# Gate, up and router products in plain fp32, with all expert weights resident in SBUF

## What is computed

```
logits = (x @ wt.T + repeat(g @ wg.T)) / 2             # 8 experts
scores = softmax(logits);  topk_w, topk_idx = top_k(scores, 2), normalised
gp = leaky(einsum('th,ehm->etm', x, w_gate))           # H = 256, M = 128
up = einsum('th,ehm->etm', x, w_up)
y_all = einsum('etm,emh->eth', gp * up, w_down)
y = sum of topk_w * y_all over the two chosen experts
p = leaky(x @ sw_gate) * (x @ sw_up) @ sw_down         # shared, width 256
y = y + p
```

## Time and profile before

| | us |
|---|---|
| runs: median, lowest, highest | 1060.24, 1060.23, 1061.74 |
| the profiled execution's own time | 1064.17 |
| its span, first to last instruction | 1062.4 |
| PE busy | 1014.6 (96%) |
| DVE busy | 707.4 (67%) |
| ACT busy | 526.5 (50%) |

### The profile page before, as it was taken

One profiled execution on the slowest core, in us unless ns is written; L12 is line 12 of the kernel. 1 busy time (PEld: TensorE's weight loads), 2 busy tenths in 40 slices (PEclk: granted clock), 3 DMA queues, 4 the chain that ended last, 5 costly groups with the idle time before them and its releaser, 6 DMA issues.

```text
span 1062.4 us, 21427 instructions
## 1 busy us (share of the span) xinstructions
PE 1014.6 (96%) x6788; PEld 815.3 (77%) x6788; DVE 707.4 (67%) x2457; ACT 526.5 (50%) x1564; POOL 437.0 (41%) x422
## 2 busy tenths in 40 slices
PE   3887999999999999999999999999999999999998
PEld 2665877778777887778777787777877788777877
DVE  8789577665867558665676647676576755856543
ACT  3488346651565435663456614665246643565220
POOL 1634154441554333642535515454245534444212
PEclk9899999999999999999999999999999999999999
DMA  5316414112132013311132212311123211232043
GB/s 198 80 54 215 151 60 122 53 66 63 61 110 90 28 55 101 100 61 61 43 118 72 71 42 79 112 65 46 62 66 113 82 41 41 84 106 71 20 138 102
DMA packets 40996, 87.68 MB, mean 83 GB/s; under 512 B 4192, under 2 KB 19040, under 8 KB 40624
## 3 DMA queue, kind: packets, MB, share of 16 engines
q1 hardware_dynamic: 39920, 83.57, 24.5%
q10 hardware_dynamic: 960, 2.62, 0.7%
HBM read 76.57 MB, written 9.60 MB: 81 GB/s over the span
## 4 chain that ended last, share of the span: by engine, by line
PE 75%; DVE 10%; issue 5%; ACT 4%; DVEq 0%; POOL 0%; ACTq 0%
PE psY L1641 13%; PE psS L1511 6%; PE psO L1547 5%; PE psG L69 5%; PE psG L71 5%; PE psG L70 5%; PE psT L1522 5%; PE psS L71 3%; PE psS L70 3%; PE psS L69 3%; PE psS L1507 3%; PE psT L1529 2%; PE psO L1550 2%; PE psT L69 2%; PE psT L71 2%
## 5 line engine op out<-in xcount | busy, mean ns | idle before, releaser
L604 POOL TENSOR_TENSOR work<-work,rden 128x514 f32<-128x514 f32 x128 | 134.0, 1047 | 322.3 <-DVE rden L1137 321.6
L1641 PE MATMUL psY<-Wd,H 128*128 128x256 f32 x640 | 172.5, 399 | 0.0
L763 ACT ACTIVATE work<-work,low 128x257 f32<-128x257 f32 x256 | 128.5, 504 | 60.1 <-DVE low L1155 59.5
L69 PE MATMUL psG<-x1T_hi,Wgu 128*128 128x512 f32 (+1 forms) x292 | 134.8, 462 | 2.6 <-ACT leaky L807 1.9
L1641 PEld LDWEIGHTS psY<-Wd,H 128*128 128x128 f32 x640 | 112.4, 190 | 29.4 <-issue 14.4
L1155 DVE CUSTOM_DVE_ANT_0 work<-psS,bias,null_s 128x256 f32<-128x256 f32 x256 | 113.3, 480 | 28.4 <-PE psS L1511 25.9
L1251 DVE SCALAR_TENSOR_TENSOR leaky<-leaky 128x512 f32<-128x512 f32 x80 | 56.4, 704 | 101.5 <-ACT leaky L807 100.5
L71 PE MATMUL psG<-x1T_lo,Wgu 128*128 128x512 f32 (+1 forms) x292 | 114.9, 394 | 0.0
L70 PE MATMUL psG<-x1T_hi,Wgu 128*128 128x512 f32 (+1 forms) x292 | 114.4, 392 | 0.0
L593 POOL TENSOR_TENSOR rq<-qss,neghalf 128x16 f32<-128x16 f32 x32 | 97.5, 3048 | 36.3 <-DVE qss L1131 36.3
L1511 PE MATMUL psS<-KB,qT 64*128 64x256 f32 (+1 forms) x1024 | 105.7, 325 | 0.0
(11 more groups left out here) (259 smaller groups left out, 2306.7 us busy)
## 6 DMA issues: line engine op xcount, KB each, us to landing
Wgu<-wexp SPq DMA_DIRECT2D x80, 512.0 KB, 3.4
Wb<-wscr SPq DMA_DIRECT2D x64, 256.0 KB, 3.6
wexp<-Wgu SPq DMA_DIRECT2D x10, 512.0 KB, 2.9
xres<-in_x SPq DMA_DIRECT2D x8, 512.0 KB, 4.7
xin<-in_x SPq DMA_DIRECT2D x7, 512.0 KB, 4.2
out<-work SPq DMA_DIRECT2D x7, 512.0 KB, 2.9
H<-in_wgu SPq DMA_DIRECT2D x10, 256.0 KB, 3.9
bias<-bscr SPq DMA_DIRECT2D x4, 512.0 KB, 6.6
```

What stands on the lines that cost most here:

```text
L69: te.matmul(dst, a_hi, b_hi, start=start, stop=False)
L604: pool.tensor_tensor(T1[sl][:, hs, :], T1[sl][:, hs, :], rden[sl][:, 1, hs].unsqueeze(2) .to_broadcast([P, 2, N + 1]), ALU.mult)
L763: act.activation(T1[sl][:, h, :], T1[sl][:, h, :], ACT.Exp, scale=-1.0, bias=low[sl][:, 1, h:h + 1], accum_out=den[sl][:, 1, h:h + 1])
L1641: mm = te.matmul(psY[:, t // 2, (t % 2) * D:(t % 2 + 1) * D], H[:, k % H_RING, t * P:(t + 1) * P], Wd[:, ORDER[k], :], start=(k == 0 and t ...
```

## The change

Gate, up and the router's logits become plain fp32 matmuls. x1T is one fp32 tile: ACT copies its half 0, DVE its half 1. Wgu holds all ten blocks (20 KB per partition) and is loaded once, by ten DMAs of 256 KB straight from the input. The splitting in round 0, `wexp`, `load_weights` and all its waits go; the fp32r copy of the router's weights, the identity sum I2 and the logits' second half of rows go as well. One wait is added on PE, in round 0, behind the query products.

```diff
-        x1T = [sb(f"x1T_{part}", [P, KC, TOK], F32R) for part in PARTS]
-        Wgu = sb("Wgu", [P, W_RING, 2, 2, KC, P], F32R)
+        x1T = sb("x1T", [P, KC, TOK])
+        Wgu = sb("Wgu", [P, BLOCKS, 2, KC, P])
...
-            for e in range(BLOCKS + 2):
-                if e < BLOCKS:
-                    if e >= H_RING:
-                        sp.wait_ge(parts_done.sem, e - H_RING + 1)
-                    sp.dma_start(H[:, e % H_RING, :], wgu[e].rearrange("p w c m -> p (w c m)")) \
-                        .then_inc(wraw_in[e % H_RING].sem, 16)
-                if e >= 2:
-                    sp.wait_ge(parts_done.sem, e - 1)
-                    sp.dma_start(wexp.ap()[e - 2], Wgu[:, (e - 2) % W_RING].bitcast(F32)) \
-                        .then_inc(parts_out[(e - 2) % W_RING].sem, 16)
+            for k in range(BLOCKS):
+                sp.dma_start(Wgu[:, k], wgu[ORDER[k]]).then_inc(ld_gu.sem, 16)
...
-                        act.activation(Wgu[:, e % W_RING, 0], H[:, e % H_RING, :].rearrange(
-                            "p (w c m) -> p w c m", w=2, c=KC), ACT.Copy).then_inc(lead_done.sem, 1)
...
-                for c, bank in ((0, psG), (1, psO)):
-                    need(act, x1T_ps, m, c + 1)
-                    act.activation(x1T[0][:, c, :], bank[:], ACT.Copy).then_inc(x1T_a.sem, 1)
+                need(act, x1T_ps, m, 1)
+                act.activation(x1T[:, 0, :], psG[:], ACT.Copy).then_inc(x1T_a.sem, 1)
...
-                        dve.tensor_tensor(Wgu[:, e % W_RING, 1], H[:, e % H_RING, :].rearrange(
-                            "p (w c m) -> p w c m", w=2, c=KC), Wgu[:, e % W_RING, 0].bitcast(F32),
-                            ALU.subtract).then_inc(parts_done.sem, 1)
...
-            def x1_parts(m):
-                for c, bank in ((0, psG), (1, psO)):
-                    need(dve, x1T_a, m, c + 1)
-                    dve.tensor_tensor(x1T[1][:, c, :], bank[:], x1T[0][:, c, :].bitcast(F32),
-                                      ALU.subtract).then_inc(x1T_v.sem, 1)
+            def x1_turned(m):
+                need(dve, x1T_ps, m, 2)
+                dve.tensor_copy(x1T[:, 1, :], psO[:]).then_inc(x1T_v.sem, 1)
...
                 if moe is None:
                     te.wait_ge(ld_down.sem, 16)
+                if moe is None:
+                    te.wait_ge(ld_gu.sem, 16 * BLOCKS)
                 need(te, kb_a, r, 1)
...
-                need(te, x1T_v, m, 2 * KC if last else KC)
+                need(te, x1T_a, m, 2 if last else 1)
+                need(te, x1T_v, m, 2 if last else 1)
                 for c in range(KC):
-                    te.matmul(logit_bank(last), WtP[:, c, :], x1T[0][:, c, :], start=(c == 0), stop=False, skip_group_check=True)
-                for c in range(KC):
-                    mm = te.matmul(logit_bank(last)[0:E, :], WtP[:, c, 0:E], x1T[1][:, c, :], start=False, stop=(c == KC - 1),
-                                   skip_group_check=True)
+                    mm = te.matmul(logit_bank(last), Wt[:, c, :], x1T[:, c, :], start=(c == 0), stop=(c == KC - 1))
...
             def gate_up(m, k, w, bank):
                 for c in range(KC):
-                    mm = products(te, bank, [Wgu[:, k % W_RING, part, w, c, :] for part in range(2)],
-                                  [part[:, c, :] for part in x1T], c == 0, c == KC - 1)
+                    mm = te.matmul(bank, Wgu[:, k, w, c, :], x1T[:, c, :], start=(c == 0), stop=(c == KC - 1))
```

More of the change, by code:

```diff
@@ L51 @@
 WOUT_AT = (3, 4)
-SPLIT_AT = 6
 LAST_DOWN = 18
@@ L287, in logit_bank @@
         def logit_bank(last):
-            return psY[0:2 * E, 1, :] if last else psO[0:2 * E, :]
+            return psY[0:E, 1, :] if last else psO[0:E, :]
         def weight_bank(last):
@@ L330, in attention_moe @@
         bias_in = [events(f"bias_in{i}", 0) for i in range(BIAS_PARTS)]
[L331 to L334, removed]
+        ld_gu = events("ld_gu", 0)
         xin_in = events("xin_in", 16)
@@ L478, in load_round @@
                 sp.dma_start(xres[:], x_t[r]).then_inc(xres_in.sem, 16)
[L480 to L485, removed]
             def experts(m):
-                for k in range(W_RING, 2 * W_RING):
-                    load_weights(m, k)
                 need(sp, hw_done, m - 1, E)
@@ L778, in route @@
             def route(m):
[L779 to L781 removed]
+                need(act, x1T_ps, m, 1)
+                act.activation(x1T[:, 0, :], psG[:], ACT.Copy).then_inc(x1T_a.sem, 1)
             def route_half(m, half):
[L784 to L787 removed]
+                need(act, x1T_ps, m, KC * half + 1)
+                act.activation(x1T[:, 0, half_tokens(half)], psT[:, 0, half_tokens(half)], ACT.Copy) \
+                    .then_inc(x1T_a.sem, 1)
             def logits(m, last=False):
@@ L906, in kv_parts @@
             def kv_parts():
[L907 to L910, removed]
+                hi, lo = (part[:, :, KV0:Q0] for part in Wall)
+                pre(dve.tensor_copy(hi, Wkvn_in))
+                pre(dve.tensor_tensor(lo, Wkvn_in, hi.bitcast(F32), ALU.subtract))
                 n = wall_trail(slice(0, KC), Q0, 2 * P)
@@ L1232, in router_weights @@
                 ch.end()
-            def x1_parts(m):
-                for c, bank in ((0, psG), (1, psO)):
-                    need(dve, x1T_a, m, c + 1)
-                    dve.tensor_tensor(x1T[1][:, c, :], bank[:], x1T[0][:, c, :].bitcast(F32),
-                                      ALU.subtract).then_inc(x1T_v.sem, 1)
+            def x1_turned(m):
+                need(dve, x1T_ps, m, 2)
+                dve.tensor_copy(x1T[:, 1, :], psO[:]).then_inc(x1T_v.sem, 1)
             def x1_half(m, half):
-                for c in range(KC):
-                    need(dve, x1T_a, m, KC * half + c + 1)
-                    dve.tensor_tensor(x1T[1][:, c, half_tokens(half)], psT[:, c, half_tokens(half)],
-                                      x1T[0][:, c, half_tokens(half)].bitcast(F32), ALU.subtract).then_inc(x1T_v.sem, 1)
+                need(dve, x1T_ps, m, KC * half + 2)
+                dve.tensor_copy(x1T[:, 1, half_tokens(half)], psT[:, 1, half_tokens(half)]).then_inc(x1T_v.sem, 1)
             def leak(m, k):
@@ L1565, in turn_half @@
                 if half > 0:
-                    need(te, x1T_v, m, KC * half)
+                    need(te, x1T_a, m, half)
+                    need(te, x1T_v, m, half)
                 for c in range(KC):
@@ L1572, in block_half @@
             def block_half(m, k, w, half):
-                need(te, wgu_ld[k % W_RING], m, 16 * (k // W_RING + 1))
-                need(te, x1T_v, m, KC * (half + 1))
+                need(te, x1T_a, m, half + 1)
+                need(te, x1T_v, m, half + 1)
                 cols = half_tokens(half)
@@ L1578, in block_half @@
                 for c in range(KC):
-                    mm = products(te, bank[:, cols], [Wgu[:, k % W_RING, part, w, c, :] for part in range(2)],
-                                  [part[:, c, cols] for part in x1T], c == 0, c == KC - 1)
+                    mm = te.matmul(bank[:, cols], Wgu[:, k, w, c, :], x1T[:, c, cols], start=(c == 0), stop=(c == KC - 1))
                 return mm
             def logits(m, last=False):
-                need(te, x1T_v, m, 2 * KC if last else KC)
+                need(te, x1T_a, m, 2 if last else 1)
+                need(te, x1T_v, m, 2 if last else 1)
                 for c in range(KC):
-                    te.matmul(logit_bank(last), WtP[:, c, :], x1T[0][:, c, :], start=(c == 0), stop=False, skip_group_check=True)
-                for c in range(KC):
-                    mm = te.matmul(logit_bank(last)[0:E, :], WtP[:, c, 0:E], x1T[1][:, c, :], start=False, stop=(c == KC - 1),
-                                   skip_group_check=True)
+                    mm = te.matmul(logit_bank(last), Wt[:, c, :], x1T[:, c, :], start=(c == 0), stop=(c == KC - 1))
                 mm.then_inc(lt_ps.sem, 1)
```

45 lines of the change are left out of this document (9 added, 36 removed).

## The result

The changed kernel takes 1122.05 us (median; 1120.89 to 1122.33) against 1060.24: a ratio, over all runs, of 1.0578, 95% interval 1.0560 to 1.0596. That is 61.8 us more, where 67 were forecast, and inside the range. The profiled executions differ by 58.0 in their spans (1062.4 and 1120.4): the one of before lay 3.9 above its median.

The account below looks back on a forecast made before the run. The prediction took PE's queue of matmuls to bound the merged rounds. Longer products +62.1, swallowed waits -7.3, round 0's split -5.5 and its new wait +18 gave +67.3 on the median 1060.24: 1127 us, range 1110 to 1145.

Parts of the forecast that it names:

- The pace of plain fp32 at 512 columns: Gate and up on PE: 0.43 us per record, 1.72 per product where 1.37 stood, 0.35 us more each.
- The rivals on this pace: Gate and up: a plain fp32 record of 512 columns takes 0.23 us, kernel about 1001 us; chance 0.04.
- weight loads in the open: Plain fp32 matmuls on PE: weight loads not hidden over 688 records, 83 us more, 1210 us; chance 0.05.
- The router: Router's logits on PE: two plain matmuls take 1.72 us for 0.93, 0.79 more a round, 6.3 in all.
- What the waits swallow: PE's waits shrink behind longer products: 0.9 us a merged round, 6.3, plus 1.0 in the final stage, 7.3 less.
- Round 0, the new wait: PE waits for all ten weight blocks before turning round 0's queries: 18 us more, bounds +15 to +23.
- Round 0, the split: Round 0's loop loses ten ACT and ten DVE splitting passes: 5.5 us less.
- The last merged round and the final stage: Longer products and router, less swallowed waits, at the kernel's end: 13.5 us more, 6.9 and 6.6.
- Weights in time: Rival for round 0: loads beat PE to its wait or cost nothing extra, +49.3, 1110 us; chance 0.13.
- 131 ns a matmul: Skill page's pace at 512 columns: sum on PE about 45 us in place of 62; given no chance.

Follow-up runs that it names:

- its own run: Weights loaded early and their wait late, as in the 1103.85 us run, but the router's product back to four fp32r passes over leading parts: 1096.15 us.
- the lengthened body: Changed kernel with weights loaded early and their wait late, plus 48 long-met waits in TensorE's loop body: 1107.26 us, 3.4 more than without them.
- the moved wait: Changed kernel with TensorE's wait for the ten weight loads moved behind round 0's loop: 1103.68 us, 18.4 less than the changed kernel.
- the two runs with shortened bodies: Kernel before with implied or repeated TensorE waits removed, loop body 1771 or 1759 instructions: 1061.10 against 1060.03 us, and 1060.37 against 1059.67.
- fewer waits: Kernel before with 32 implied TensorE waits per round taken out, loop body 1771 instructions: 1061.10 us against 1060.03.
- the split in the gaps: Kernel before with six of ten blocks split early, the subtractions on VectorE in its idle times before the first score: 1061.78 us against 1060.37.

## Why the prediction was right, step by step

- **The pace of plain fp32 at 512 columns**: 0.43 per record was forecast by scaling, 0.43 it is. From the start of a down product to the transposes behind the gate, 2.69 us now; before, 2.35 (450.85 to 453.20). Over whole steps of the loop, with one gate or up in each, two steps grew from 9.65 us (427.02 to 436.67) to 10.31 (454.00 to 464.31). So 0.33 to 0.34 per product, against 0.35. The rivals on this pace and on weight loads in the open fall with these rows. Before, then after:

```profile
427.02 1.13 PE L1641 MATMUL psY<-Wd,H 128*128 128x256 f32 x4
...
436.67 1.13 PE L1641 MATMUL psY<-Wd,H 128*128 128x256 f32 x4
...
450.85 1.13 PE L1641 MATMUL psY<-Wd,H 128*128 128x256 f32 x4
...
453.20 0.60 PE L1522 MATMUL psT<-ident,work 128*128 128x128 f32 x4
```

```profile
454.00 1.13 PE L1573 MATMUL psY<-Wd,H 128*128 128x256 f32 x4
...
464.31 1.13 PE L1573 MATMUL psY<-Wd,H 128*128 128x256 f32 x4
```

- **The router**: 0.79 a round forecast; 0.88 in the trace, 7.7 us in all by its own run, against 6.3. The old router's steps were read rightly; plain fp32 gave 1.81, not 1.72: its records start 0.43 apart, and the gate behind them starts 0.52 after the last.
- **What the waits swallow**: the term that failed. "That can be the 0.9 for DVE and the 0.3 for ACT, not the 0.6 before x1, ahead of which nothing grew", and 0.9 a round was taken. All 1.8 us of the earlier trace rows went. That nothing grew ahead of x1 was right; but the gap was no wait on work at all. The change cut TensorE's loop body from 1803 to 1718 instructions, and the round stopped fetching code. This is the larger part of why a merged round came to 131.1 where the forecast's sum gives 132.6 (its text said 133), and why 61.8 us came out in place of 67: the five repeated gaps are worth 3.4 by the lengthened body. The smaller part is the pace: 20 products at 0.33 are 6.6, not 7.0. With these, 6.6 + 0.9 - 1.8 = 5.7 against the 5.4 measured; some 0.3 us per round stay unplaced.
- **Round 0, the new wait**: +18 forecast, 18.4 by the moved wait. The mechanism was right; that the number fits so well is partly luck, for two parts were off and made up for each other. TensorE resumed at 61.8, not 64, and needed 6.3 us from there to the first score, not 7.2, so that came 16.7 late, not 19.8. But the forecast then took 1.8 off, most of it for the clock. Against the run with the moved wait, whose first score comes at 51.0, the changed kernel lost 17.1 up to its own and some 1.3 more from there to the next turning of tokens (60.1 against 58.7), with its clock at half once more (111.8 to 115.2).
- **Round 0, the split**: -5.5 forecast. Passes taken out alone gave 2.4 to 5.5 by the interval, 3.2 in the medians, and 5.9 in the profiled loop, one half-clock stretch included. From the first score to the next turning of tokens, executions with one such stretch in between can be compared: 62.8 and 63.1 us in the two runs with shortened bodies, which have the passes, and 60.1 in the changed kernel. That is 2.7 to 3.0 us, so the forecast was most likely 2 to 3 us too high.
- **The last merged round and the final stage**: 13.5 forecast (6.9 and 6.6), 11.9 measured. The difference is the profiled execution of before, whose clock was at half from 1019.9 to 1023.3, behind the router's wait: its last part, from round 7's turning of tokens to the end, takes 193.8 us. In the runs with fewer waits and with the split in the gaps, the same work at a granted clock of 1.00, it takes 192.1 and 192.3, and the changed kernel's 205.8 is 13.4 to 13.7 more.
- **"Weights in time"**, the rival at 1110: it was wrong for this order of the program, but one moved wait makes it true, and better: 1103.7. The forecast stood on where the wait was written, not on the transfers: the ten loads are in some 15 us after the first is issued in either place (46.5 to 61.8 and 11.3 to 27.0).
- By the 131 ns a matmul of the Trainium skill's page "TensorE: Matmul & The Clock Gate", section "Back-to-back issue gap", the sum on TensorE would have been 45 us, as an estimate, and the time near 1110. The rows here do not agree: at 512 columns an fp32r record takes 228 ns and a plain fp32 record 429.

## What to carry to other kernels

Where a product is split into three fp32r passes because TensorE is the bound, plain fp32 was no saving here: four column times against three (1.72 us a gate against 1.37), and the splitting on other engines that it spares is worth a few microseconds once. Put a wait for data in front of its first use, not where the code happens to be convenient: here that placement alone cost 18 us of the 62. A gap put down to "issue" at the head of a loop body is worth a look at the instruction queue's packets before it is called a wait.

## What was not expected of the hardware

The loop body's code is fetched again in every round, in 16.4 KB packets, once it reaches past a certain point: with 1718 instructions ending at the 3262nd of TensorE's program (and with 1759 ending at the 3264th) there are 20 or 21 packets in all, with 1771 ending at the 3285th and with 1766 ending at the 3310th there are 66. The first turn of x1 behind the jump back then starts 0.3 to 1.1 us later. Whether the end's place relative to a packet's border decides, or the length, these runs don't tell apart for certain.
